# Attention over graph edges on one core: the order of TensorE's and ScalarE's work within a slot of 512 edges

## The chip, the cores and the metric

The kernel runs on one core of a Trainium2 chip. The metric is device time in microseconds (us) for one execution of the whole program, as the median over runs. Lower is better.

## What is computed

The reference is one layer of a graph model on 1250 nodes of 768 features: two rounds of graph attention (GATv2) over 41,250 edges, a linear-attention mixer and a feed-forward block. The change lies in the graph attention, of which this is the core:

```python
hs = (x @ Ws + bs).reshape(N, H, HD)
hd = (x @ Wd + bd).reshape(N, H, HD)
hs_e = hs[src]
e = jax.nn.leaky_relu(hs_e + hd[dst], SLOPE)
logits = jnp.einsum('ehd,hd->eh', e, attn)
m = jax.ops.segment_max(logits, dst, num_segments=N)
ex = jnp.exp(logits - m[dst])
s = jax.ops.segment_sum(ex, dst, num_segments=N)
alpha = ex / s[dst]
out = jax.ops.segment_sum(alpha[..., None] * hs_e, dst, num_segments=N)
```

## The kernel before, in words

The edges are sorted by destination and cut into tiles of 128. Four tiles make a macro of 512 edges, and there are 91 macros in each of the two rounds (function `attend`, called twice). Each macro passes through three steps, and the steps of three successive macros are worked on together in one slot:

- **turn** (of macro m+1): the 512 gathered source rows (`rows[b]`, 128 edges by 800 columns for each tile) are turned, so that features lie on partitions, in six chunks of 128 features. For each tile of a chunk, TensorE makes two instructions into the same 128x128 piece of a PSUM bank (`turned`): a bf16 product that places the destination's row (`dst_rows` by `place`, the "place product", L559) and a transpose of the source rows that is added to it (L561). A chunk fills a bank of 512 columns. There are four banks, so a chunk waits until ScalarE has taken the chunk four before it. ScalarE takes a chunk with a Relu into `relu[c]` (function `bend`, L502, 128x512).
- **head** (of macro m): TensorE sums the bent chunks to eight scores for each edge (`sum_heads`, L574 and L578). VectorE scans them for running maxima (`scan_left`, `scan_right`, L659 and L664) and subtracts them (`shift`, L668). TensorE turns the scores back (`turn_back`, L584), and ScalarE makes the weights of them (`weights`, L512). ScalarE also makes `rise` and `drop` (L506, L508), TensorE sums the drops (`sum_drops`, L589), and ScalarE makes the `factors` of them by which older sums shrink (L518, four instructions). VectorE spreads the weights over 1024 columns (`spread_out`, L676).
- **message** (of the macro whose head step was in the slot before): TensorE multiplies spread weights by rows (`messages`, L597), and VectorE adds the results to the sums, scaled by the factors (`add_total`, L686, eight instructions).

The order in each engine's queue is written out by hand, in a function `slot` for each engine, and it is the same in every slot. On TensorE it is: messages, chunk 0, heads, chunks 1 to 3, turn back, chunk 4, sum of drops, the linear part (L568), chunk 5. On ScalarE: bend 0, bend 1, rise and drop, weights, bends 2 to 4, factors, bend 5. On VectorE (untouched by the change): line up (L647), join (L653, two instructions), the eight adds, copy of an index, the two scans, shift, and small work, then the spreading. GpSimd gathers rows by indirect DMA (L483), and SyncE loads the places and flags.

What waits for what around the change: the adds wait for all four factors of their macro and for the earlier adds (L682 to L684); heads wait for the bends and for the joins; `turn_back` waits on TensorE's sequencer for the shift (L583); the spreading waits for the weights; the messages wait for the spreading.
Of the kernel before, what the change touches and what calls it, by code (L numbers as in the profile page):

```python
# [15 lines left out]
P = 128  # L16
# [15 lines left out]
G = 4  # L32
# [369 lines left out]
def attend(layer, ahead, sums, table, local_rows, run_flags, src_index, dst_local, first_dst, still_first, block_of, sum_of,  # L402
           iota_row, split_of, ident, head_rows, quarter_mask, dst_rows, sems, nc, **_):

    with ExitStack() as ctx:
# [32 lines left out]
        def chunk(b, c):  # L438
            return (b * KC + c) % BANKS
# [7 lines left out]
        with nc.Block() as block:  # L447
# [48 lines left out]
            @block.scalar  # L496
            def _(act):
                def bend(m, b, c, first=False):
                    if not first:
                        act.wait_ge(heads_done, m)  # L500
                    act.wait_ge(turned_done, m * KC + (c + 1))
                    act.activation(relu[c][:], turned[chunk(b, c)][:], ACT.Relu, scale=attn_size[:, c:c + 1]).then_inc(bent, 1)  # L502

                def drops(m, b):
                    act.wait_ge(scanned, m * SCANS + (SCANS + 2))
                    act.activation(rise[:], left[(b + 1) % 2][:, P - 1:P], ACT.Identity, bias=right[:, 0:1], scale=-1.0).then_inc(raised, 1)  # L506
                    act.wait_ge(raised, m + 2)
                    act.activation(drop[:], quarter_mask[:, 0], ACT.Relu, scale=rise[:]).then_inc(dropped, 1)  # L508

                def weights(m):  # L510
                    act.wait_ge(turned_back, 2 * m + 1)
                    act.activation(weight[:].rearrange("p (j h) -> p j h", j=G), back[:, 0:P].rearrange("p (j r) -> p j r", j=G)[:, :, 0:H],  # L512
                                   ACT.Exp).then_inc(weights_ready, 1)

                def factors(m, b):
                    act.wait_ge(turned_back, 2 * m + 2)
                    for j in range(G):
                        act.activation(factor[b % 2][:, j, :], back[:, P + j * HH:P + (j + 1) * HH], ACT.Exp,  # L518
                                       scale=first_dst[:, bass.ds(m * G + j, 1)]).then_inc(weights_ready, 1)

                def slot(turn, head, first=False, fresh=False):
                    if turn:
                        bend(turn[0], turn[1], 0, first)
                        bend(turn[0], turn[1], 1, first)
                    if head:
                        drops(head[0], head[1])
                        weights(head[0])
                    if turn:
                        bend(turn[0], turn[1], 2, first)
                        bend(turn[0], turn[1], 3, first)  # L530
                        bend(turn[0], turn[1], 4, first)
                    if head:
                        factors(head[0], head[1])
                    if turn:
                        bend(turn[0], turn[1], 5, first)

                act.sem_inc(bent, BANKS)  # L537
                slot(macro(0, 0), None, first=True)
                slot(macro(0, 1), macro(0, 0))
                with act.Fori(0, LOOPS) as i:  # L540
                    for b in range(UNROLL):
                        slot(macro(i, b + 2), macro(i, b + 1))
                slot(macro(LOOPS, 2), macro(LOOPS, 1))
                slot(None, macro(LOOPS, 2))
                act.wait_ge(merged, 1)
                for j in range(1, G):
                    act.activation(merge[:, j], back[:, 0:2 * G * HH].rearrange("p (s j k) -> p j s k", s=2, j=G)[:, j], ACT.Exp,
                                   scale=first_dst[:, j:j + 1]).then_inc(merge_seen, 1)

            @block.tensor  # L550
            def _(pe):
                def turn_chunk(m, b, round, at, c):
                    if c == 0:
                        pe.wait_ge(gathered[b], landed(layer, b, round + 1))
                        pe.wait_ge(place_ready, m + 1)
                    pe.wait_ge(bent, m * KC + (c + 1))
                    for j in range(G):
                        into = turned[chunk(b, c)][:, j * P:(j + 1) * P]
                        pe.matmul(into, dst_rows[0:SP_ROWS, bass.ds(at[j], 1), c * P:(c + 1) * P].rearrange("p o d -> p (o d)"),  # L559
                                  place[b][:, j * P:(j + 1) * P], start=True, stop=False)  # L560
                        last = pe.matmul(into, rows[b][:, j, c * P:(c + 1) * P], ident[:],  # L561
                                         is_transpose=True, start=False, stop=True)
                    last.then_inc(turned_done, 1)

                def turn_linear(m):
# [35 lines left out]
                def slot(turn, head, message):  # L601
                    if turn:
                        at = places_of(nc, mybir.EngineType.PE, block_of, turn[0], 1)
                    if message:
                        for pair in range(2):
                            messages(message[0], message[1], pair)
                    if turn:
                        turn_chunk(*turn, at, 0)
                    if head:
                        sum_heads(head[0], head[1])  # L610
                    if turn:
                        for c in range(1, 4):
                            turn_chunk(*turn, at, c)
                    if head:
                        turn_back(head[0])
                    if turn:
                        turn_chunk(*turn, at, 4)
                    if head:
                        sum_drops(head[0])
# [1670 lines left out]
```

## Time and profile before

| | |
|---|---|
| runs shown | 2255.08, 2255.70, 2258.92 us; median 2255.7 |
| profiled execution | span 2250.3 us from its first to its last instruction; a time of its own around that span isn't given |
| busy share | PE 96%, PEld 75%, DVE 75%, ACT 50%, POOL 40% |
| place products (L559) | 4368, two groups of 407.7 and 394.1 us busy |
| transposes (L561) | 4368, two groups of 427.9 and 413.3 us busy |
| granted TensorE clock | mean 0.986 |

PE is TensorE's array and PEld its weight loads, which overlap with it. Matmuls overlap each other, so their lengths do not add up to time: what counts is the distance from one start to the next. The letter q behind an engine's name is its sequencer, which runs ahead of the engine.

### The profile page before, as it was taken

How to read it: one execution, taken by the hardware profiler on the slowest of the kernel's cores; microseconds unless marked ns; L12 is line 12 of the kernel's file. 1: busy time of each engine (PE TensorE's matmuls, PEld its weight loads, DVE VectorE, ACT ScalarE, POOL GpSimd, SP SyncE). 2: the span in 40 equal slices, each digit the busy share in tenths (PEclk: the TensorE clock that was granted, in tenths of full speed). 3: DMA queues.
4: the chain of work that ended last, by engine and by line, in shares of the span. 5: the costliest groups of instructions: out<-in, count | busy, mean ns of one | idle time of the engine just before them, and what ended most of it. 6: DMA issues, size and time to landing. Idle time of an engine off the chain costs nothing. (4 is left out here: it accounts for less than half of the span.)

```text
span 2250.3 us, 86767 instructions
## 1 busy us (share of the span) xinstructions
PE 2154.9 (96%) x31007; PEld 1684.2 (75%) x31007; DVE 1678.2 (75%) x4435; ACT 1133.4 (50%) x2749; POOL 896.5 (40%) x849
## 2 busy tenths in 40 slices
PE   8999999998999999999997999899999999999798
PEld 4665555555888888888886655688888888888676
DVE  5546872344888888888887755588888888888884
ACT  1101200034666666666664314566666666666584
POOL 0000001022666566666652211466656656656121
PEclk9999999999999999999998999999999999999899
DMA  5002044144777777787774024587777777777421
GB/s 192 1 0 71 20 142 133 57 131 133 249 250 247 249 250 243 248 252 239 247 245 153 29 97 132 168 252 242 251 242 248 240 245 250 244 246 238 171 88 48
DMA packets 143398, 404.07 MB, mean 180 GB/s; under 512 B 21811, under 2 KB 81625, under 8 KB 143073
## 3 DMA queue, kind: packets, MB, share of 16 engines
q0 software_dynamic: 59584, 298.64, 41.0%
q1 hardware_dynamic: 79691, 93.00, 13.8%
q10 hardware_dynamic: 3828, 7.85, 1.0%
q8 instruction: 264, 4.33, 0.8%
q14 instruction: 31, 0.25, 0.0%
HBM read 370.77 MB, written 17.17 MB: 172 GB/s over the span
## 5 line engine op out<-in xcount | busy, mean ns | idle before, releaser
L502 ACT ACTIVATE at_relu<-at_turned,ah_attn_size 128x512 f32<-128x512 f32 x1092 | 716.2, 692 | 392.0 <-PE at_heads L578 363.4
L483 POOL DMA_INDIRECT at_rows<-table,ah_index x360 | 404.6, 1124 | 269.0 <-DVE ah_index L696 158.5
L483 POOL DMA_INDIRECT ah_room<-table,ah_index x352 | 399.8, 1136 | 260.8 <-DVE ah_index L696 174.3
L561 PE MATMUL at_turned<-ident,ah_room 128*128 128x128 f32 x2208 | 427.9, 280 | 2.3 <-issue 2.3
L559 PE MATMUL at_turned<-ah_place,dst_rows 96*128 96x128 bf16 x2208 | 407.7, 223 | 23.4 <-ACTq L537 19.2
L561 PE MATMUL at_turned<-ident,at_rows 128*128 128x128 f32 x2160 | 413.3, 277 | 1.7 <-issue 1.4
L559 PE MATMUL at_turned<-at_place,dst_rows 96*128 96x128 bf16 x2160 | 394.1, 222 | 2.2 <-issue 1.5
L686 DVE SCALAR_TENSOR_TENSOR sums<-sums,at_factor,at_total 128x97 f32 x1456 | 343.7, 310 | 1.4 <-DVE at_gap L751 0.7
L561 PEld LDWEIGHTS at_turned<-ident,ah_room 128*128 128x128 f32 x2208 | 318.1, 144 | 26.2 <-issue 1.7
L561 PEld LDWEIGHTS at_turned<-ident,at_rows 128*128 128x128 f32 x2160 | 307.8, 143 | 24.5 <-issue 2.2
L676 DVE TENSOR_TENSOR at_spread<-at_lined,at_weight 128x1024 f32<-128x1024 f32 x182 | 223.3, 1227 | 127.7 <-ACT at_weight L512 127.7
L559 PEld LDWEIGHTS at_turned<-ah_place,dst_rows 96*128 x2208 | 224.1, 103 | 60.6 <-issue 60.5
L653 DVE SCALAR_TENSOR_TENSOR at_relu<-at_relu,ah_pair_sign 128x512 f32<-128x512 f32 x364 | 256.3, 746 | 0.0
L559 PEld LDWEIGHTS at_turned<-at_place,dst_rows 96*128 x2160 | 217.4, 103 | 36.8 <-issue 36.6
L597 PE MATMUL at_total<-at_rows,at_spread 128*32 128x100 f32 x5760 | 144.3, 253 | 1.9 <-DVE at_spread L676 1.8
L597 PE MATMUL at_total<-ah_room,at_spread 128*32 128x100 f32 x5888 | 145.7, 251 | 0.3 <-issue 0.2
L597 PEld LDWEIGHTS at_total<-ah_room,at_spread 128*32 128x32 f32 x5888 | 125.6, 110 | 12.3 <-DVE at_spread L676 2.4
L597 PEld LDWEIGHTS at_total<-at_rows,at_spread 128*32 128x32 f32 x5760 | 124.5, 111 | 13.2 <-DVE at_spread L676 3.9
L518 ACT ACTIVATE at_factor<-at_back,first_dst 128x2 f32<-128x2 f32 x728 | 132.8, 283 | 1.1 <-PE at_back L589 1.1
L578 PE MATMUL at_heads<-at_relu,ah_sign_mask 128*8 128x128 f32 x2912 | 116.5, 273 | 1.6 <-issue 1.4
L574 PE MATMUL at_heads<-at_relu,ah_sign_mask 128*8 128x128 f32 x2912 | 114.0, 273 | 0.2 <-issue 0.2
L1748 ACT ACTIVATE pr_parts<-pr_dst_row 128x384 bf16<-128x384 f32 x60 | 31.2, 522 | 124.9 <-DVEq L1845 112.0
(317 smaller groups left out, 3179.7 us busy)
## 6 DMA issues: line engine op xcount, KB each, us to landing
at_flags<-run_flags SPq DMA_DIRECT2D x182, 64.0 KB
dst_rows<-pr_parts SPq DMA_DIRECT2D x76, 144.0 KB, 2.6
ah_place<-local_rows SPq DMA_DIRECT2D x92, 96.0 KB
at_place<-local_rows SPq DMA_DIRECT2D x90, 96.0 KB
table<-ah_room SPq DMA_DIRECT2D x20, 400.0 KB, 2.4
ah_room<-table,ah_index POOLq DMA_INDIRECT x368
at_rows<-table,ah_index POOLq DMA_INDIRECT x360
mx_w<-in_L_mix_W_qkv SPq DMA_DIRECT2D x4, 1152.0 KB, 11.8
```

The costliest lines, as they stand in the source:

```text
L483: pool.indirect_dma_start(rows[b][:, j, :], None, table, bass.IndirectOffsetOnAxis(index[b][:, j:j + 1], 0)).then_inc(gathered[b], 16)
L502: act.activation(relu[c][:], turned[chunk(b, c)][:], ACT.Relu, scale=attn_size[:, c:c + 1]).then_inc(bent, 1)
L518: act.activation(factor[b % 2][:, j, :], back[:, P + j * HH:P + (j + 1) * HH], ACT.Exp, scale=first_dst[:, bass.ds(m * G + j, 1)]).then_in ...
L559: pe.matmul(into, dst_rows[0:SP_ROWS, bass.ds(at[j], 1), c * P:(c + 1) * P].rearrange("p o d -> p (o d)"), place[b][:, j * P:(j + 1) * P], ...
L561: last = pe.matmul(into, rows[b][:, j, c * P:(c + 1) * P], ident[:], is_transpose=True, start=False, stop=True)
L574: pe.matmul(head_row(j), sign_mask[:, c, :], relu[c][:, j * P:(j + 1) * P], start=False, stop=False)
L578: last = pe.matmul(head_row(j), sign_mask[:, c, :], relu[c][:, j * P:(j + 1) * P], start=False, stop=c == JOINED[-1][1])
L597: last = pe.matmul(part(j)[h % HM * S:(h % HM + 1) * S, h // HM, :], spread[:, j, h, :], rows[b][:, j, :].rearrange("p (g h r) -> p h g r" ...
L653: dve.scalar_tensor_tensor(relu[c][:], relu[from_][:], pair_sign[:, c:c + 1], relu[c][:], ALU.mult, ALU.add).then_inc(joined, 1)
L676: dve.tensor_tensor(spread[:], lined[:].unsqueeze(2).broadcast_to([P, G, H, S]), weight[:].rearrange("p (j h) -> p j h", j=G).unsqueeze(3) ...
L686: dve.scalar_tensor_tensor(into[:, k], into[:, k], factor[b % 2][:, j, k:k + 1], part(j)[:, k, 0:HW], ALU.mult, ALU.add).then_inc(added, 1)
L1748: act.activation(heads_half(parts[t % 2][:, s, :], half), heads_half(dst_row[:], half), ACT.Copy).then_inc(split_done, 1)
```

## The change

The change does three things in `attend`. TensorE makes the four place products of a chunk in a row and then the four transposes, instead of alternating (and only the first of a bank carries the start flag). TensorE makes the heads directly behind the messages, ahead of chunk 0, and turns back behind chunk 2 instead of chunk 3. ScalarE makes bend 5 ahead of the factors instead of behind them.

```diff
@@ scalar: slot
                         bend(turn[0], turn[1], 4, first)
+                        bend(turn[0], turn[1], 5, first)
                     if head:
                         factors(head[0], head[1])
-                    if turn:
-                        bend(turn[0], turn[1], 5, first)
@@ tensor: turn_chunk
                     pe.wait_ge(bent, m * KC + (c + 1))
+                    into = [turned[chunk(b, c)][:, j * P:(j + 1) * P] for j in range(G)]
                     for j in range(G):
-                        into = turned[chunk(b, c)][:, j * P:(j + 1) * P]
-                        pe.matmul(into, dst_rows[0:SP_ROWS, bass.ds(at[j], 1), c * P:(c + 1) * P].rearrange("p o d -> p (o d)"),
-                                  place[b][:, j * P:(j + 1) * P], start=True, stop=False)
-                        last = pe.matmul(into, rows[b][:, j, c * P:(c + 1) * P], ident[:],
-                                         is_transpose=True, start=False, stop=True)
+                        pe.matmul(into[j], dst_rows[0:SP_ROWS, bass.ds(at[j], 1), c * P:(c + 1) * P].rearrange("p o d -> p (o d)"),
+                                  place[b][:, j * P:(j + 1) * P], start=j == 0, stop=False)
+                    for j in range(G):
+                        last = pe.matmul(into[j], rows[b][:, j, c * P:(c + 1) * P], ident[:],
+                                         is_transpose=True, start=False, stop=j == G - 1)
                     last.then_inc(turned_done, 1)
@@ tensor: slot
-                    if turn:
-                        turn_chunk(*turn, at, 0)
                     if head:
                         sum_heads(head[0], head[1])
                     if turn:
-                        for c in range(1, 4):
+                        for c in range(3):
                             turn_chunk(*turn, at, c)
                     if head:
                         turn_back(head[0])
                     if turn:
+                        turn_chunk(*turn, at, 3)
                         turn_chunk(*turn, at, 4)
```

On TensorE, from the messages to the heads, one slot of the kernel before reads so (ISA is the register instruction, `x16` and `x4` count equal rows):

```order
L597 MATMUL at_total1_0<-ah_room,at_spread_0 32x100 x16
L559 ISA
L559 MATMUL at_turned0_0<-at_place2_0,dst_rows 128x128
L561 MATMUL at_turned0_0<-ident,at_rows2_0 128x128
L559 ISA
L559 MATMUL at_turned0_0<-at_place2_0,dst_rows 128x128
L561 MATMUL at_turned0_0<-ident,at_rows2_0 128x128
...
L574 MATMUL at_heads_0<-at_relu4_0,ah_sign_mask 8x128 x4
L574 MATMUL at_heads_0<-at_relu5_0,ah_sign_mask 8x128 x4
```

The same place in the changed kernel (whose place products stand on line 558):

```order
L597 MATMUL at_total1_0<-ah_room,at_spread_0 32x100 x16
L574 MATMUL at_heads_0<-at_relu4_0,ah_sign_mask 8x128 x4
L574 MATMUL at_heads_0<-at_relu5_0,ah_sign_mask 8x128 x4
L578 MATMUL at_heads_0<-at_relu1_0,ah_sign_mask 8x128 x4
L578 MATMUL at_heads_0<-at_relu3_0,ah_sign_mask 8x128 x4
L558 ISA
L558 MATMUL at_turned0_0<-at_place2_0,dst_rows 128x128
...
L561 MATMUL at_turned0_0<-ident,at_rows2_0 128x128 x4
```

The heads now stand next to the messages, and each chunk has four register instructions and products ahead of four transposes. On ScalarE, from the weights to the factors in an early slot of the kernel before:

```order
L512 ACTIVATE at_weight_0<-at_back_0 128x32
L502 ACTIVATE at_relu2_0<-at_turned0_0,ah_attn_size 128x512
L502 ACTIVATE at_relu3_0<-at_turned1_0,ah_attn_size 128x512
L502 ACTIVATE at_relu4_0<-at_turned2_0,ah_attn_size 128x512
L518 ACTIVATE at_factor0_0<-at_back_0,first_dst 128x2 x4
L502 ACTIVATE at_relu5_0<-at_turned3_0,ah_attn_size 128x512
```

And in the changed kernel:

```order
L512 ACTIVATE at_weight_0<-at_back_0 128x32
L502 ACTIVATE at_relu2_0<-at_turned0_0,ah_attn_size 128x512
L502 ACTIVATE at_relu3_0<-at_turned1_0,ah_attn_size 128x512
L502 ACTIVATE at_relu4_0<-at_turned2_0,ah_attn_size 128x512
L502 ACTIVATE at_relu5_0<-at_turned3_0,ah_attn_size 128x512
L518 ACTIVATE at_factor0_0<-at_back_0,first_dst 128x2 x4
```

The four factors moved behind bend 5, which reads the last chunk that TensorE turns in the slot.

## Rows read from the trace of the kernel before

**Rows 1.** Busy time by stretch; columns: busy us of each engine, clock, DMA share, GB/s
```profile
560.00:1200.00 640.00, 635.28 (x12853) 556.78 (x12846) 560.75 (x1652) 430.15 (x1127) 392.00 (x346) 1.00 0.78 247
1440.00:2140.00 700.00, 677.01 (x13706) 592.33 (x13705) 606.87 (x1771) 461.02 (x1197) 396.24 (x354) 0.99 0.75 239
```

**Rows 2.** The same view for line 559 alone: PE and PEld busy (count)
```profile
620.00:1150.00 530.00, 315.58 (x1728) 173.95 (x1728) 1.00 0.78 247
1560.00:2050.00 490.00, 288.52 (x1581) 159.25 (x1580) 1.00 0.78 245
```

**Rows 3.** Timeline of PE over one slot: start us, length us, instruction
```profile
802.22 0.28 PE L561 MATMUL at_turned<-ident,at_rows 128*128 128x128 f32 x1
802.42 1.58 PE L597 MATMUL at_total<-at_rows,at_spread 128*32 128x100 f32 x64
803.94 0.23 PE L559 MATMUL at_turned<-ah_place,dst_rows 96*128 96x128 bf16 x1
...
804.52 0.28 PE L561 MATMUL at_turned<-ident,ah_room 128*128 128x128 f32 x1
804.73 0.62 PE L574 MATMUL at_heads<-at_relu,ah_sign_mask 128*8 128x128 f32 x16
805.17 0.62 PE L578 MATMUL at_heads<-at_relu,ah_sign_mask 128*8 128x128 f32 x16
805.73 0.23 PE L559 MATMUL at_turned<-ah_place,dst_rows 96*128 96x128 bf16 x1
...
807.65 0.22 PE L559 MATMUL at_turned<-ah_place,dst_rows 96*128 96x128 bf16 x1
807.71 0.28 PE L561 MATMUL at_turned<-ident,ah_room 128*128 128x128 f32 x1
807.82 0.27 PE L584 MATMUL at_back<-ident,at_shifted 128*128 128x128 f32 x1
807.93 0.22 PE L559 MATMUL at_turned<-ah_place,dst_rows 96*128 96x128 bf16 x1
...
808.63 0.29 PE L589 MATMUL at_back<-at_drop,head_rows 128*128 128x8 f32 x2
808.77 0.31 PE L568 MATMUL at_heads<-ident,at_linear 128*128 128x128 f32 x1
808.92 0.22 PE L559 MATMUL at_turned<-ah_place,dst_rows 96*128 96x128 bf16 x1
```

**Rows 4.** Timeline of PE near the end: six transposes of one kind in a row
```profile
2146.09 0.82 PE L2092 MATMUL fi_turned<-ident,nodes 128*128 128x128 f32 x6
```

**Rows 5.** Timeline of ACT over the slot
```profile
802.66 0.73 ACT L518 ACTIVATE at_factor<-at_back,first_dst 128x2 f32<-128x2 f32 x4
803.24 0.73 ACT L502 ACTIVATE at_relu<-at_turned,ah_attn_size 128x512 f32<-128x512 f32 x1
...
808.13 0.20 ACT L512 ACTIVATE at_weight<-at_back 128x32 f32<-128x32 f32 x1 [0.30 <-issue]
808.23 1.84 ACT L502 ACTIVATE at_relu<-at_turned,ah_attn_size 128x512 f32<-128x512 f32 x3
809.94 0.73 ACT L518 ACTIVATE at_factor<-at_back,first_dst 128x2 f32<-128x2 f32 x4
```

**Rows 6.** Timeline of DVE over the slot
```profile
802.66 1.41 DVE L653 SCALAR_TENSOR_TENSOR at_relu<-at_relu,ah_pair_sign 128x512 f32<-128x512 f32 x2
803.99 1.89 DVE L686 SCALAR_TENSOR_TENSOR sums<-sums,at_factor,at_total 128x97 f32 x8
806.84 0.29 DVE L668 TENSOR_TENSOR at_shifted<-at_heads,at_right 128x128 f32<-128x128 f32 x1
808.36 1.23 DVE L676 TENSOR_TENSOR at_spread<-at_lined,at_weight 128x1024 f32<-128x1024 f32 x1 [0.67 <-ACT at_weight L512]
```

**Rows 7.** Sequencers, by line: L683 and L686 (DVE), L583 and L559 (TensorE); last numbers: first and last start
```profile
L683 DVEq FUSED_REGOPS  x1: 46/46/46, 803.5 to 803.5; - x1
L686 DVEq FUSED_REGOPS  x4: 57/60/64, 803.6 to 804.1; - x4
L583 PEldq EVENT_SEMAPHORE  x1: 51/51/51, 807.2 to 807.2; - x1
L559 PEldq FUSED_REGOPS  x4: 46/46/46, 807.3 to 807.8; - x4
L559 PEldq FUSED_REGOPS  x12: 46/46/46, 805.0 to 806.4; - x12
```

## The prediction

> **What bounds the kernel now.** First the stretches: in the two attention rounds (about 1340 of 2250 us) PE is busy 635 of 640 and 677 of 700 us, DVE 88%, ACT 67%, and DMA 78%, at full clock [rows 1]. So TensorE's order decides there. Then the length of a slot. A slot has 24 place products, so the counts of line 559 give 72 slots in 530 us and 65.9 in 490 us, or 7.36 and 7.44 us each [rows 2]. The timeline of an undisturbed slot has 7.28 us: it starts with the messages at 802.42 and its last chunk, as long as the others, ends 0.78 us behind 808.92, at 809.70 [rows 3]. The difference, some 0.12 us a slot or 22 us over 182 slots, is scattered pauses that the change doesn't touch.
>
> I write times within the slot from its messages (0.00). TensorE [rows 3]: messages 0.00, chunk 0 at 1.52, heads 2.31, chunk 1 at 3.31, turn back 5.40, chunk 4 at 5.51, drops 6.21, linear 6.35, chunk 5 at 6.50, next slot 7.28. DVE [rows 6]: joins 0.24 to 1.65, eight adds 1.57 to 3.46, shift done 4.71, then 0.67 us idle until the spreading at 5.94 (done 7.17, just ahead of the next messages). ACT [rows 5]: weights at 5.71, bends 2 to 4 end 7.65, factors 7.52 to 8.25, that is 0.24 to 0.97 of the next slot, where the adds use them at 1.57.
>
> **Heads behind the messages: a gain on PE.** A start-to-start distance of 0.21 us stands between the last transpose and the heads (804.52 to 804.73), and as much between transpose and messages, where a transpose is otherwise followed after 0.11 (807.71 to 807.82) [rows 3]. The change of shape thus costs about 0.1 us, and there are four in a slot. Heads next to messages leave two. I take 0.1 off at the first (heads at 1.42) and 0.1 for the chunk that no longer ends in a change: 0.2 us a slot. Bounds: 0.1, if going from 32 columns to 8 costs as much as the others, and 0.2.
>
> **Place products in a row: a small gain.** A pair takes 0.174 us (0.06 from place product to transpose, 0.114 from there to the next) and a chunk 0.695 [rows 3]. Six like transposes in a row start (0.82-0.27)/5 = 0.11 us apart [rows 4]. Nothing shows a place product behind another; it can hardly take longer than the 0.06 to a transpose whose weights are larger. With 0.056 to 0.06, a chunk takes 0.67 to 0.695 us. I take 0.675. [...]
>
> If PE were all that counts, the slot would be 7.28 - 0.2 - 6x0.02 = 6.96 us.
>
> **Bend 5 ahead of the factors: a new loop.** Bend 5 reads chunk 5, the last of TensorE's slot. Its last transpose starts 0.20 ahead of the next messages and lasts 0.28 (802.22) [rows 3], so it is done at 0.08 of the next slot. Bend 5 starts at about 0.11 and takes 0.69 (it was one of three in 1.84, which overlap a little [rows 5]): it ends at 0.80. The four factors start 0.12 ahead of that, as they do behind bend 4 (808.23+1.84 against 809.94), and take 0.73: done at **1.41**, not 0.97. In exchange nothing is won: the heads read bend 5 at 1.42 at the earliest and had it at 1.55 when they stood at 2.31 [rows 3, 5].
>
> The adds wait for all four factors, and this wait stands in DVE's sequencer (L683), which passed it at 803.5, with the first register instruction of the adds 0.1 later and another 0.1 until an add can start [rows 7]. So the first add starts at 1.41+0.03+0.2 = **1.64**, where it was 1.57. It can't be earlier however early the joins end. Behind it nothing changes on DVE: from the first add to the end of the shift are 807.13-803.99 = 3.14 us [rows 6]. The shift is done at 4.78, and what is queued behind the adds (index copy, scans) is as late.
>
> **Turn back behind chunk 2: a new wait.** TensorE arrives there at 2.42 (heads 1.42, as long as before 1.00) + 3x0.675 = 4.45, against 5.40 before. The wait for the shift stands in TensorE's sequencer (L583), which passed it at 807.2, less than 0.1 behind the end of the shift at 807.13 [rows 6, 7]. With 0.04 it is released at 4.82. Before, there were 0.66 us from this release to the turn back at 807.82, in which the sequencer made the next register instructions. Now there is nothing between. These come 0.125 us apart (eleven distances in 1.4 us [rows 7]), more slowly than place products run (0.06), and in a row none is hidden behind a transpose. The four of chunk 3 come 0.125 to 0.50 behind the release, and the fourth product can't start before its register instruction has run (0.046 us, and as much again for the way to the engine, my estimate): 4.82+0.59 = 5.41. The engine alone would have been there at 4.45+0.11+0.17 = 4.73. So PE stands still for about 0.68 us a slot in two pieces, before the turn back and in the place products of chunk 3. In other chunks the sequencer is ahead: it has the heads' 1.00 us to prepare chunk 0.
>
> Sum: fourth product 5.41, rest of chunk 3 0.06+3x0.11+0.114 = 0.50, chunk 4 0.675, drops and linear 0.29, chunk 5 0.675, change of shape 0.09: the next slot starts at **7.64**. The other loop (turn back 4.93, weights by 5.5, spreading done 6.75) isn't late. Each slot hands the same times to the next, so this holds throughout: +0.36 us a slot.
>
> About 178 slots have all three steps: +64 us. Part of the 22 us of pauses falls before the turn back, where PE now waits anyway (4.45 of 7.28 of the slot); about 10 us of them are swallowed. Net +54 us, on a span of 2250.3. The median of the runs is 5.4 above this span, and I keep that: 2255.7+54 = **2310 us**. Work outside the rounds isn't touched. The gathers are triggered by the index copy, 0.07 later in a longer slot, and get more time, so DMA costs nothing; it is at 78% and falls.
>
> **The rivals.**
> - *The sequencer's pitch does not show.* Register instructions without transposes between them may go through faster than 0.125 us. Then only the wait for the shift is left: turn back at 4.93, and 0.11+3x0.675+0.29+0.09 behind it gives 7.45. +0.17x178 = 30, less 10: about 2276. For it: nothing shows four register instructions with a single product between them. Against: they kept 0.125 whatever lay between.
> - *PE stays the bound* (the other side): the slot is then 6.96 to 7.1 and the kernel 32 to 57 us faster, 2199 to 2224. Place and price: this decides at the first add. If it started 0.6 us earlier than I have it, at about 1.0, the release would come at 4.2 and TensorE would find its instructions ready. For it: DVE has 0.67 us of idle time per slot, which an earlier turn back turns into earlier joins. Against: the joins don't decide; the factors do, and they can't be done before 1.41 as they stand behind a bend that stands behind chunk 5.
> - *The halves cancel*: a slot of 7.2 to 7.3, if the factors come sooner than I count and the pitch shows only partly. Within 0.2% of before, about what a measurement of this kernel can tell from no change.
> - *Place products in a row are slow.* By the worst bound that a row gives (0.11 us each, as a transpose), chunks 4 and 5 grow by 3x0.055 each: 7.97 a slot, some 2369. Nothing in the rows supports it, as a product after a product loads less. [...]
>
> **How the numbers follow.** The forecast as worked out has 0.52 (2295 to 2325, with add, release and chunk each off by a few hundredths), the unseen pitch 0.22, slow place products 0.06: slower 0.80. PE as the bound 0.14, cancelling 0.06. The range leaves out the faster cases and the slowest: 2266 to 2327.
>
> **What would show it.** Right: slots of about 7.6 us; in ACT's timeline the factors directly behind bend 5 and done 1.4 behind the messages; the first add 1.6 behind them, with DVE idle before it and released by ACT's factors; idle PE before the turn back and in chunk 3, released by DVE's shift or "issue"; the spreading no longer just ahead of the messages; PE's share below 93% in the rounds. Wrong: adds at 1.3 or earlier, PE without idle time before the turn back, or slots under 7.28. Apart from the sum, heads 1.42 behind the messages and chunks of 0.675 would confirm the two small gains.

## The result, and the profile after

The changed kernel takes 2312.85 us (median of 4 runs, 2311.01 to 2314.47) against 2256.64 us before in the same comparison: a ratio of 1.0248 (95% interval 1.0232 to 1.0264). It is slower by 56 us; the forecast was 2310 us. The profiled execution has a span of 2312.5 us.

The busy time by stretch, with the columns of [rows 1]; the second line starts later, as the whole second round does:

```profile
560.00:1200.00 640.00, 605.78 (x12259) 540.82 (x12257) 536.46 (x1568) 429.83 (x1073) 419.76 (x331) 1.00 0.79 235
1480.00:2180.00 700.00, 657.23 (x13239) 585.89 (x13241) 586.43 (x1723) 466.69 (x1166) 438.45 (x349) 1.00 0.76 226
```

PE was busy 635 of the first 640 us [rows 1] and is now busy 606, or 95%. It has gained idle time, at an unchanged granted clock of 1.00. The same view for the line of the place products, as in [rows 2]:

```profile
620.00:1150.00 530.00, 175.92 (x1648) 129.59 (x1648) 1.00 0.79 235
1560.00:2050.00 490.00, 162.38 (x1516) 119.44 (x1516) 1.00 0.79 236
```

24 products make a slot, so 68.7 and 63.2 slots: 7.72 and 7.76 us each, where it was 7.36 and 7.44. Over 182 slots these are 62 us, as much as the spans of the two profiled executions differ (2312.5 against 2250.3): the whole loss lies in the slots of the two rounds.

PE's timeline over one undisturbed slot, to be laid beside [rows 3] (undisturbed means without a scattered pause; `...` stands for rows left out):

```profile
1064.42 0.61 PE L561 MATMUL at_turned<-ident,at_rows 128*128 128x128 f32 x4
1064.95 1.58 PE L597 MATMUL at_total<-at_rows,at_spread 128*32 128x100 f32 x64
1066.35 0.62 PE L574 MATMUL at_heads<-at_relu,ah_sign_mask 128*8 128x128 f32 x16
...
1067.34 0.40 PE L558 MATMUL at_turned<-ah_place,dst_rows 96*128 96x128 bf16 x4
1067.57 0.60 PE L561 MATMUL at_turned<-ident,ah_room 128*128 128x128 f32 x4
1068.02 0.39 PE L558 MATMUL at_turned<-ah_place,dst_rows 96*128 96x128 bf16 x4
...
1069.89 0.30 PE L584 MATMUL at_back<-ident,at_shifted 128*128 128x128 f32 x1 [0.37 <-DVE at_first_max L670]
1070.03 0.58 PE L558 MATMUL at_turned<-ah_place,dst_rows 96*128 96x128 bf16 x4
1070.44 0.61 PE L561 MATMUL at_turned<-ident,ah_room 128*128 128x128 f32 x4
1070.89 0.39 PE L558 MATMUL at_turned<-ah_place,dst_rows 96*128 96x128 bf16 x4
...
1072.60 0.29 PE L597 MATMUL at_total<-at_rows,at_spread 128*32 128x100 f32 x4
```

Both small gains are there: the heads start 1.40 behind the messages, and a chunk takes 0.67 to 0.68 (1067.34 to 1068.02), later 0.66. Then the turn back comes at 4.94, with idle PE before it. The row of four place products behind it takes 0.58 us instead of 0.39: this is the second piece of standstill. No idle column shows it, since each product lasts 0.22 us and the next starts 0.12 us behind it. The slot is 1072.60 - 1064.95 = 7.65 us. It is one of the shorter ones: of the 67 whole slots between 620 and 1150 us the median is 7.71, and the longer ones differ mostly in that same row, which takes up to 0.1 more.

The profile names `at_first_max` as what the turn back waited for. That is the instruction behind the shift on DVE; the shift itself ended at 1069.74 (below), and the wait was passed at 1069.8. Over the window of 620 to 1150 us the waits view has this row, and the kernel before has none such:

```profile
PE at_back L584 <- DVE at_first_max L670: 19.9, 54, 0.4
```

ACT's and DVE's timelines of that slot:

```profile
1065.06 0.69 ACT L502 ACTIVATE at_relu<-at_turned,ah_attn_size 128x512 f32<-128x512 f32 x1 [0.27 <-PE at_turned L561]
1065.65 0.71 ACT L518 ACTIVATE at_factor<-at_back,first_dst 128x2 f32<-128x2 f32 x4
```

```profile
1064.33 1.41 DVE L652 SCALAR_TENSOR_TENSOR at_relu<-at_relu,ah_pair_sign 128x512 f32<-128x512 f32 x2
1066.60 1.90 DVE L685 SCALAR_TENSOR_TENSOR sums<-sums,at_factor,at_total 128x97 f32 x8 [0.86 <-PE at_total L597]
1069.45 0.29 DVE L667 TENSOR_TENSOR at_shifted<-at_heads,at_right 128x128 f32<-128x128 f32 x1
1070.45 1.22 DVE L675 TENSOR_TENSOR at_spread<-at_lined,at_weight 128x1024 f32<-128x1024 f32 x1
```

Bend 5 waits for PE's last transpose (0.11 behind the messages), and the factors are done at 1.41. DVE has finished its joins at 0.8 and sits idle for 0.86 us. Its adds start at 1.65 and the shift ends at 4.79. The profile puts that idle time down to PE's messages (at_total). The sequencers' rows say otherwise:

```profile
L681 DVEq ALU_OP  x1: 40/40/40, 1065.9 to 1065.9; - x1
L682 DVEq FUSED_REGOPS  x1: 46/46/46, 1066.4 to 1066.4; - x1
L583 PEldq EVENT_SEMAPHORE  x1: 51/51/51, 1069.8 to 1069.8; - x1
L558 PEldq FUSED_REGOPS  x4: 46/46/46, 1069.9 to 1070.3; - x4
```

None of DVE's rows is a wait itself, so when a wait was passed is read from the first row behind it. Behind the wait for the messages' first half (line 679) that is L681. It starts at 0.97, 0.07 us behind the end of the last message of that half, in all 67 whole slots between 620 and 1150 us. Behind the wait for the factors (line 681) it is L682. It starts at 1.44 or 1.45, 0.04 us behind the end of the last factor (1066.36 in this slot), in all 67, and the first add follows 0.21 us later. So the factors came last. On TensorE the wait for the shift has a row of its own, L583, which starts 0.04 us behind the end of the shift in 66 of the 67 slots, here at 1069.8. The four register instructions of chunk 3 come only behind it, the first 0.13 us later. In the same window no two register instructions of L558 start less than 0.12 us apart, and no place product starts less than 0.10 us behind its own. The fourth product of chunk 3 stands at this limit, 0.10 us behind its register instruction in the median slot.

### The profile page after: what moved, and what is told of

It reads as the page before. It is cut to its first block and busy times, and to the rows that moved or that the text cites. A ratio compares the mean times of both kernels' runs of the same rounds, so it can differ in the third digit from the quotient of the medians.

```text
span 2312.5 us, 86767 instructions
## 1 busy us (share of the span) xinstructions
PE 2157.4 (93%) x31007; PEld 1708.0 (74%) x31007; DVE 1683.8 (73%) x4435; ACT 1178.4 (51%) x2749; POOL 991.2 (43%) x849
## 5 line engine op out<-in xcount | busy, mean ns | idle before, releaser
L483 POOL DMA_INDIRECT ah_room<-table,ah_index x352 | 449.0, 1275 | 247.3 <-DVE ah_index L695 163.1
L561 PE MATMUL at_turned<-ident,ah_room 128*128 128x128 f32 x2208 | 338.1, 276 | 0.8 <-issue 0.8
L561 PE MATMUL at_turned<-ident,at_rows 128*128 128x128 f32 x2160 | 327.6, 274 | 0.0
L558 PE MATMUL at_turned<-ah_place,dst_rows 96*128 96x128 bf16 x2208 | 237.7, 221 | 20.1 <-ACTq L536 19.3
L561 PEld LDWEIGHTS at_turned<-ident,ah_room 128*128 128x128 f32 x2208 | 235.1, 142 | 1.0 <-issue 0.9
L558 PE MATMUL at_turned<-at_place,dst_rows 96*128 96x128 bf16 x2160 | 231.3, 220 | 1.8 <-issue 1.2
L561 PEld LDWEIGHTS at_turned<-ident,at_rows 128*128 128x128 f32 x2160 | 227.7, 141 | 0.0
L558 PEld LDWEIGHTS at_turned<-ah_place,dst_rows 96*128 x2208 | 175.1, 99 | 58.1 <-issue 42.7
L558 PEld LDWEIGHTS at_turned<-at_place,dst_rows 96*128 x2160 | 170.0, 98 | 38.7 <-issue 23.7
L584 PE MATMUL at_back<-ident,at_shifted 128*128 128x128 f32 x182 | 53.9, 296 | 58.9 <-DVE at_first_max L670 58.4
```

The source lines that it names most:

```text
L483: pool.indirect_dma_start(rows[b][:, j, :], None, table, bass.IndirectOffsetOnAxis(index[b][:, j:j + 1], 0)).then_inc(gathered[b], 16)
L558: pe.matmul(into[j], dst_rows[0:SP_ROWS, bass.ds(at[j], 1), c * P:(c + 1) * P].rearrange("p o d -> p (o d)"), place[b][:, j * P:(j + 1) * ...
L561: last = pe.matmul(into[j], rows[b][:, j, c * P:(c + 1) * P], ident[:], is_transpose=True, start=False, stop=j == G - 1)
L584: pe.transpose(back[:, 0:P], shifted[:], ident[:]).then_inc(turned_back, 1)
```

## The experiments

State of the theory before them. **A**: the slot is set by a loop: last chunk, bend 5, factors, adds, scans, release of the turn back, then the sequencer's pitch, then the rest of the chunks. **B**: turning back behind chunk 2 is too early for VectorE, whatever ScalarE does. **S**: the register instructions don't matter, only the wait.

### 1. Bend 5 behind the factors again (in the changed kernel)

```diff
-                        bend(turn[0], turn[1], 5, first)
                     if head:
                         factors(head[0], head[1])
+                    if turn:
+                        bend(turn[0], turn[1], 5, first)
```

> The changed kernel with bend 5 behind the factors again, all else as changed. Theory A (the loop chunk 5, bend 5, factors, adds, scans, turn back decides): the factors are done about 0.5 us behind the messages, the adds start as soon as the joins are done, the release of the turn back moves from 4.8 to about 4.4 and the slot falls from 7.64 to about 7.1 us: 2216 to 2235 us. Rival B (turning back behind chunk 2 is too early for VectorE whatever ScalarE does, the bend's place is without effect): the first add stays near 1.6, slots of 7.5 us or more, 2285 us or more.

Measured: 2263.38 us, ratio to before 1.0027 (1.0016 to 1.0037), in neither of the expected ranges. The place of one activation is worth 49 us of the 56. B alone is refuted. But the gain that A promised beyond that did not come. The slot from 959.36 to 966.61 has 7.25 us and not 7.1. The rows of PE, DVE and DVE's sequencer there:

```profile
959.36 1.58 PE L598 MATMUL at_total<-at_rows,at_spread 128*32 128x100 f32 x64
963.98 0.27 PE L585 MATMUL at_back<-ident,at_shifted 128*128 128x128 f32 x1
966.61 0.29 PE L598 MATMUL at_total<-at_rows,at_spread 128*32 128x100 f32 x4
```

```profile
960.62 1.89 DVE L686 SCALAR_TENSOR_TENSOR sums<-sums,at_factor,at_total 128x97 f32 x8 [0.31 <-PE at_total L598]
...
963.46 0.29 DVE L668 TENSOR_TENSOR at_shifted<-at_heads,at_right 128x128 f32<-128x128 f32 x1
```

```profile
L682 DVEq ALU_OP  x1: 40/40/40, 960.3 to 960.3; - x1
```

The joins end at 0.94 and the factors earlier, yet the adds start at 1.26. Now it is the wait for the messages' first half that comes last: the first row behind it (L682 in this kernel) starts at 0.965 in all 70 whole slots of the window, 0.07 us behind the end of that half, while the factors are done at 0.45 in the median. I had left it out: the adds have a floor at 1.26, so the release has one at 4.44, and 2.8 us behind it make 7.25. The loop is still there, with the messages as its first member in place of bend 5 and the factors. In this slot TensorE itself came late (turn back at 4.62 with no wait, behind a row of place products in chunk 0 that took 0.62 us). In 52 of the 70 whole slots of the window the turn back stands at 4.54 to 4.56, just behind the release. The first add stands at 1.26 or 1.27 in all of them, and no slot is shorter than 7.25.

### 2. Turn back behind chunk 3 (in the changed kernel)

```diff
-                        for c in range(3):
+                        for c in range(4):
                             turn_chunk(*turn, at, c)
                     if head:
                         turn_back(head[0])
                     if turn:
-                        turn_chunk(*turn, at, 3)
                         turn_chunk(*turn, at, 4)
```

> The changed kernel with the turn back behind chunk 3 instead of chunk 2; bend 5 stays ahead of the factors. Both theories have TensorE arrive at about 5.05, behind the release at 4.8. Theory A with the sequencer's pitch: adds still at 1.62 and the shift still at 4.79, but they are covered now. Bound by turn back to messages over weights and spreading (1.88 us): slots of 6.94 us, 2190 to 2205 us, some 110 us faster than the changed kernel and some 55 faster than the kernel before. If bend 5 costs by itself, without a wait at the turn back, the slot stays above 7.2: 2245 us or more.

Measured: 2238.18 us, ratio 0.9908 (0.9892 to 0.9925), 75 us faster than the changed kernel and 33 us above the expected range. The late factors, which are still there, don't hold the kernel up any more; they cost together with a turn back that comes before the release. The best slots are near the expected 6.94 (messages at 919.31 and 926.31, 7.00 us), but the mean is 530/(1740/24) = 7.31 us. The missing 40 us are in the difference between the two, and it has two parts. One is scattered pauses, which experiments 5 to 11 take up. The other is the sequencer's pitch again. The turn back stands at 5.07, at most 0.24 behind the release (4.83), so the register instructions of the row behind it aren't all ready: the fourth starts 0.27 us behind the turn back in the median slot, where the first product starts 0.11 us behind it. In 51 of the 71 whole slots of the window the fourth place product of that row starts 0.21 us or more behind the first, where 0.17 is normal, and the median slot has 7.14 us.

### 3. Place products and transposes in alternation again (in the changed kernel)

The diff is abbreviated; `[...]` stands for addresses that stay as they are.

```diff
                     for j in range(G):
-                        pe.matmul(into[j], dst_rows[...], place[b][...], start=j == 0, stop=False)
-                    for j in range(G):
-                        last = pe.matmul(into[j], rows[b][...], ident[:], is_transpose=True, start=False, stop=j == G - 1)
+                        pe.matmul(into, dst_rows[...], place[b][...], start=True, stop=False)
+                        last = pe.matmul(into, rows[b][...], ident[:], is_transpose=True, start=False, stop=True)
```

> The changed kernel with place product and transpose in alternation again, order of chunks, heads, turn back and bends as changed. With the sequencer's pitch of 0.125 us: the row of place products of chunk 3 no longer stands still, which gives back more than the rows had won: turn back at 4.93, then 2.58 us: slots of 7.52 us, about 2291 us, faster than the changed kernel by about 20. Without such a pitch the rows were a plain gain and taking them back makes slots of 7.70 to 7.78: 2325 to 2340 us.

Measured: 2292.21 us, ratio 1.015 (1.0133 to 1.0167): 20 us faster than the changed kernel, as the pitch demands. PE behind the turn back:

```profile
710.40 0.30 PE L583 MATMUL at_back<-ident,at_shifted 128*128 128x128 f32 x1 [0.30 <-DVE at_first_max L669]
710.53 0.22 PE L558 MATMUL at_turned<-at_place,dst_rows 96*128 96x128 bf16 x1
...
711.06 0.22 PE L558 MATMUL at_turned<-at_place,dst_rows 96*128 96x128 bf16 x1
711.12 0.28 PE L560 MATMUL at_turned<-ident,at_rows 128*128 128x128 f32 x1
711.23 0.22 PE L558 MATMUL at_turned<-at_place,dst_rows 96*128 96x128 bf16 x1
```

A pair takes 0.175, more than the pitch of 0.125 (in none of the fourteen traces do two register instructions of the place products start less than 0.12 us apart between 620 and 1150 us), so chunk 3 runs through in 0.70 us (710.53 to 711.23), where the row version took 0.86 (1070.03 to 1070.89). Rows are a gain of 0.02 to 0.035 a chunk where the sequencer is ahead, and a loss of 0.16 right behind a release. S is refuted: the wait is the same, and only the register instructions have come to stand between transposes.

### 4. The wait for the shift on the weight load

```diff
-                    pe.wait_ge(weights_ready, m * EXPS + EXPS)
                     pe.wait_ge(scanned, m * SCANS + (SCANS + 3))
+                    pe.wait_ge(weights_ready, m * EXPS + EXPS)
```

> The changed kernel with the two waits of the turn back written in the other order, so that the wait for the shift lies on the weight load in the engine's queue, and the sequencer can run ahead of it with its register instructions. If the sequencer's standstill costs the second piece: turn back still at about 4.9, but chunk 3 runs at 0.66 us behind it and the slot falls from 7.64 to about 7.43: 2272 to 2282 us. If the register instructions are not what the place products of chunk 3 wait for: no change, 2308 to 2316 us.

Measured: 2295.39 us, ratio 1.0156 (1.0139 to 1.0173). It gives 17 us instead of the expected 31 to 41. The sequencer's rows and the turn back itself:

```profile
L583 PEldq EVENT_SEMAPHORE  x1: 51/51/51, 633.6 to 633.6; - x1
L558 PEldq FUSED_REGOPS  x5: 46/46/46, 634.8 to 635.3; - x5
```

```profile
634.84 0.33 PE L584 MATMUL at_back<-ident,at_shifted 128*128 128x128 f32 x1 [0.28 <-DVE at_shifted L667]
```

The other wait, written last now, has the row L583. It was passed early, at 633.6. The wait for the shift has no row: its release shows only in the weight load and the transpose of the turn back, which both start at 634.84, 0.06 us behind the end of the shift (0.15 us in the changed kernel). The register instructions still begin only with the turn back, at 634.8, and in 59 of the 69 whole slots of the window the first of them starts 0.01 us ahead of it. That first one has a wait of its own, for a bend, but that bend was done some 4 us before. So in this place too the wait for the shift held the sequencer; my premise that it could run ahead was wrong. What is saved is the semaphore instruction (51 ns) between the release and the turn back, which stands at 4.85 instead of 4.94, and little of the row's standstill (0.53 us, where it was 0.58).

### 5 to 8. Each part alone, and a version built from them

The three parts were put into the kernel before, one at a time. Bend 5 ahead of the factors, alone (the first piece of the diff of the change):

> The kernel before with bend 5 ahead of the factors and nothing else. By the theory so far the first add moves from 1.57 to 1.62 and the shift from 4.71 to 4.79, but the turn back stands at 5.40 there, so both are covered: slots of 7.28 us, 2252 to 2262 us, no change. If the late factors cost by themselves: slots longer by 0.05 or more, 2266 us or more.

Measured: 2261.04 us, ratio 1.0015 (1.0005 to 1.0026): 3 us, hardly clear of noise. The delay is covered, as expected, though it is larger than I had it: over the window the median first add stands at 1.80, not 1.62, since bend 5 there has to wait for bend 4 and ends at 0.94, not at 0.80, and the factors are done at 1.55, not at 1.41. The shift ends at 4.94, still ahead of the turn back at 5.40.

Place products in rows, alone (the second piece):

> The kernel before with the place products of a chunk in a row and nothing else. A chunk takes 0.66 instead of 0.695 (0.055 from place product to place product). The turn back then stands at 5.26, and the spreading, 1.88 from turn back to messages, becomes the last: slots of 7.14 us. That is 25 us less; pauses of the sequencer may give 5 to 10 of them back: 2234 to 2248 us. If rows were bad for the sequencer everywhere, not only behind a late release: 2256 us or more.

Measured: 2252.19 us, ratio 0.9976 (0.9963 to 0.9989). The shortest slots are as expected (7.15 us), the time is 4 us above the range.

Heads behind the messages, chunks 0 to 3 behind them, alone:

> The kernel before with the heads directly behind the messages, chunks 0 to 3 and the turn back behind them, and nothing else (pairs, factors ahead of bend 5). Two changes of shape less are 0.2 us: turn back at 5.20, slots of 7.08 us; 36 us less, of which longer pauses take 5 to 10: 2224 to 2238 us. If going from the messages' shape to the heads' costs as much as the others, 0.1 us: slots of 7.18, 2240 to 2248 us.

Measured: 2251.17 us, ratio 0.9965 (0.9951 to 0.9978), outside both expected ranges. Both are gains, but only a fifth to a quarter of what undisturbed slots promise. These are as short as expected (7.06 us for the heads, in PE's timeline from 715.57 to 722.63). Changing from the messages' shape to the heads' costs nothing: the first head starts 0.066 us behind the last message, as a group of four messages does behind the group before it (0.066 in the median), where the first message starts 0.207 behind the transpose ahead of it. The mean slot is 530/(1708/24) = 7.45 us. PE's waits in the window of 620 to 1150 us name most of the difference of some 28 us:

```profile
PE at_turned L559 <- issue: 7.2, 11, 1.2
PE at_turned L561 <- issue: 6.0, 9, 1.2
PE at_heads L578 <- issue: 2.5, 5, 1.0
PE at_heads L574 <- issue: 1.8, 5, 0.6
```

That is 17.5 us of pauses in which PE waited for nothing that the profile shows; the kernel before had 3.1 in the same window (1.9, 0.8, 0.2 and 0.2).

**Turn back within chunk 3.** With heads first, rows, and the factors ahead of bend 5, turning back can be placed between the release (about 4.6) and the point from which weights and spreading would be last (4.99, my estimate: a slot of 6.87 for PE alone, less the 1.88 from turn back to messages):

```diff
@@ turn_chunk
                     for j in range(G):
+                        if j == 2 and between is not None:
+                            turn_back(between)
                         last = pe.matmul(into[j], rows[b]...
@@ slot
                         for c in range(3):
                             turn_chunk(*turn, at, c)
+                        turn_chunk(*turn, at, 3, head[0] if head else None)
-                    if head:
+                    elif head:
                         turn_back(head[0])
                     if turn:
-                        turn_chunk(*turn, at, 3)
                         turn_chunk(*turn, at, 4)
```

It has the bend order of experiment 1 and the order of waits of experiment 4 as well, so its gain isn't that of the new place alone. (The diff is against the changed kernel and abbreviated.)

> A version meant to be better than both: heads behind the messages, place products in rows, factors ahead of bend 5, and the turn back between the second and third transpose of chunk 3, with its wait for the shift written first. Turn back at 4.85, adds from 1.4, release at 4.6, so the rows of chunk 4 are prepared; turn back to messages 1.88 is 6.73, PE alone 6.87: undisturbed slots of 6.9 us. With the pauses that the run with the turn back behind chunk 3 had: 2210 to 2228 us. If TensorE arrives too early there as well, undisturbed slots stay at 7.1 and more, 2245 us or more.

Measured: **2210.62 us, ratio 0.9804 (0.9777 to 0.9832)**: between 1.7 and 2.2% faster than before and 102 us faster than the changed kernel, at the lower end of the expected range. PE's timeline:

```profile
708.42 1.58 PE L600 MATMUL at_total<-at_rows,at_spread 128*32 128x100 f32 x64
...
713.05 0.39 PE L564 MATMUL at_turned<-ident,ah_room 128*128 128x128 f32 x2
713.27 0.27 PE L587 MATMUL at_back<-ident,at_shifted 128*128 128x128 f32 x1
713.38 0.38 PE L564 MATMUL at_turned<-ident,ah_room 128*128 128x128 f32 x2
713.60 0.39 PE L559 MATMUL at_turned<-ah_place,dst_rows 96*128 96x128 bf16 x4
...
715.32 0.38 PE L600 MATMUL at_total<-at_rows,at_spread 128*32 128x100 f32 x8
```

The turn back stands at 4.85 with no idle time before it, and the row behind it takes 0.39 us. The slot is 6.90. In 72 of the 73 whole slots of the window that row is unhindered, against 20 of 71 in experiment 2: the shift ends at 4.54, 0.64 ahead of the row, where it ended 0.33 ahead of it there (4.85 and 5.18), and the sequencer has the time that it lacked: the fourth register instruction starts 0.21 us ahead of the row here, and 0.16 us behind its first product there.

### 9 to 11. Are the pauses waits for fetched instructions behind the gathers?

Two theories: **F**, the pauses are waits for instructions that DMA fetches, and the gathers' traffic makes them; **S** (not the S of experiments 1 to 4), they come from the sequencer's own work and don't depend on DMA. In three kernels, two of the four gathers of a macro move 64 columns instead of 800, so that the sums are formed from incomplete rows (the part in angle brackets is abbreviated):

```diff
+                        if paced and j > 1:
+                            pool.indirect_dma_start(rows[b][:, j, 0:64], None, <the table as rows of 64>, <the same index>)
```

> The kernel before, but two of the four gathers of a macro move 64 columns instead of 800 (from other rows of the table, so the outputs are not the reference's). TensorE's, ScalarE's and VectorE's instructions are the same; the gathers move little more than half. Theory F: the scattered pauses of TensorE are waits for its instructions, which are fetched by the same DMA engines as the gathers, and are seen where they are longer than the lead of the sequencer. Then they nearly vanish: slots of 7.28 us on average instead of 7.38 to 7.44, 2238 to 2250 us. Rival S: the pauses come from the sequencer's own work and don't depend on DMA: 2253 to 2262 us.

> The kernel with the heads alone moved (the run of 2251 us, undisturbed slots of 7.05 but 22 us of pauses in a window of 530 us), with the same light gathers. Theory F: the pauses fall below 5 us in the window, mean slot 7.1, 2205 to 2222 us. Rival S: pauses stay, 2240 us or more.

> The kernel with the turn back within chunk 3 (2210.6 us), with the same light gathers. Theory F: undisturbed slots of 6.89 us stay, pauses fall from 15 to below 5 us in the window: 2170 to 2188 us. Rival S: 2203 us or more.

| kernel | time with full gathers, us | with light gathers, us | DMA share, full and light | PE waits for issue in 530 us, full and light |
|---|---|---|---|---|
| before | 2258.96 | 2253.68 | 0.78, 0.51 | 3.1, 3.7 |
| heads alone | 2251.17 | 2239.23 | 0.79, 0.51 | 17.5, 13.8 |
| turn back within chunk 3 | 2210.62 | 2195.50 | 0.83, 0.56 | 12.4, 8.5 |

With light gathers the three ratios to before are 0.9987 (0.9973 to 1.0002), 0.9914 (0.9883 to 0.9946) and 0.9719 (0.9686 to 0.9751). The kernel before lies in the range of S; the two others lie between the ranges. (Their expectations put the pauses at 22 and 15 us, which was the mean slot less the undisturbed one over the window.) Taking away a third of the DMA load removes a fifth to a third of the pauses in the two faster orders and none in the kernel before. So the load of the gathers has a share at most.

F's other half, the fetching, can be looked for in the traces themselves, since the profile has a DMA queue that it calls instruction. The profile of the heads alone:

```profile
q8 instruction: 265, 4.34, 0.8%
```

These are 265 packets of 16 KB each, one in about 6 us during the rounds (92 in 530 us of the kernel before). All fourteen traces together have 343 of PE's waits for issue (those above 0.15 us) in the windows of 620 to 1150 and 1560 to 2050 us. In 340 of them PE goes on 1.2 to 1.7 us behind the landing of such a packet, although by chance it could be anything up to 6 us; the waits for the shift in the changed kernel end anywhere from 0.0 to 6.7 us behind one. That fits waits for fetched instructions and doesn't fit S, though no experiment here changed the fetching itself. A packet takes about as long with light gathers as with full ones (1.01 us against 1.04 in the heads alone, 1.09 against 1.07 in the best version, in the first window), which fits that the lighter load helped little.

The pauses grow when the messages and the heads stand together (17.5 us) and when rows take the place of pairs (8.7 us with rows alone, against 3.1). Why the same instructions in another order wait for their packets more often stays open.

### 12. Turn back behind chunk 2, alone (in the kernel before)

```diff
-                        for c in range(1, 4):
+                        for c in range(1, 3):
                             turn_chunk(*turn, at, c)
                     if head:
                         turn_back(head[0])
                     if turn:
+                        turn_chunk(*turn, at, 3)
                         turn_chunk(*turn, at, 4)
```

> The kernel before with the turn back behind chunk 2 instead of chunk 3 and nothing else (pairs, chunk 0 ahead of the heads, factors ahead of bend 5). TensorE arrives at 4.71. VectorE's adds can start at 1.25, when the first half of the messages is through, so the release can move to 4.45 to 4.6; a pair runs no faster than the sequencer, so nothing stands still behind it: undisturbed slots of 7.28, 2252 to 2264 us, no change. If turning back that early costs by itself, slots of 7.4 and more, 2275 us or more.

Measured: 2283.66 us, ratio 1.0114 (1.008 to 1.0148). I expected no change; the time lies in the other range, that of an early turn back that costs by itself. PE, then DVE, in a slot of 7.45 us (689.81 to 697.26):

```profile
692.56 0.62 PE L578 MATMUL at_heads<-at_relu,ah_sign_mask 128*8 128x128 f32 x16
694.66 0.30 PE L584 MATMUL at_back<-ident,at_shifted 128*128 128x128 f32 x1
```

```profile
691.07 1.90 DVE L687 SCALAR_TENSOR_TENSOR sums<-sums,at_factor,at_total 128x97 f32 x8
693.25 0.48 DVE L660 TENSOR_TENSOR_SCAN at_left<-at_flags,at_left,at_heads 128x128 f32<-128x128 bf16 x1 [0.20 <-PE at_heads L578]
```

The adds did start early, at 1.26, and end at 3.16. But the scan reads the heads, and these end at 692.56+0.62 = 693.18, 3.37 in the slot. The scan can't start before 3.44, which is when it started in the kernel before. So without moving the heads, an early turn back waits for them: TensorE would be there at 4.71 and turns back at 4.85. These 0.14 us, and 0.03 more from the turn back to the next place product, make the slot of 7.45 out of 7.28.

## Why the prediction was right

It was right in its mechanism, and in size closer than its terms deserve. By its own steps:

- **Heads behind the messages**: said 1.42, measured 1.40. The lower bound of 0.1 us didn't come into play.
- **Rows**: said 0.675 a chunk, measured 0.66 to 0.68. A product follows a product after 0.055 to 0.06 us (three distances of a row of 0.39 whose last product lasts 0.22). So the case of slow place products, 0.11 us apart (0.06), is refuted.
- **Bend 5**: start 0.11, factors done 1.41, both as said. Experiment 1 shows that this step carries 49 of the 56 us.
- **First add**: said 1.64, measured 1.65; **shift** 4.78 against 4.79; **turn back** 4.93 against 4.94.
- **Standstill in chunk 3**: fourth product said at 5.41, so the transposes at 5.47; the transposes start at 5.49. Experiment 3 shows the cause, and the case without the pitch (2276 us, 0.22) is refuted.
- **Slot**: 7.64 against 7.65 in an undisturbed slot, but 7.71 in the median, since the row behind the turn back is often slower than counted. Times 178, less 10 us that the pauses were to give back: 54 us said, 56 measured. That the sum is right to 2 us is partly luck: it had neither the longer rows nor the growth of the pauses.
- **PE stays the bound** (0.14): it was refused because the adds could not start at 1.0. The refusal holds, but for a reason I did not have complete. Experiment 1 took the factors away and the adds stopped at 1.26 on the messages' first half; experiment 12 shows a third guard, the heads, for the scan. I had looked only at the guard that was last in my own sum.
- **Pauses**: 22 us over the rounds, "which the change doesn't touch", of which 10 would be swallowed. The changed kernel's time came out near enough, but its waits for issue rose from 3.1 to 7.0 us in the window. As a general premise it is wrong: in the faster orders they grow to several times that.
- **Signs**: three of those named did not come. PE's share was to fall below 93% and is 95 and 94% in the two stretches, and no idle time shows in chunk 3, because part of the standstill lies under the lengths of products and transposes and counts as busy. And DVE's idle time was to be released by ACT's factors, but the profile names PE's messages; only the sequencer's rows show the factors. The others came, the spreading among them: it ends at 1071.67, 0.93 ahead of the next messages.

So the loss came from a combination. Bend 5 alone costs 3 us. Turning back earlier with heads moved, rows, and factors in their old place costs next to nothing (1.0027). Together they cost 56, and 20 of these are the rows, a gain elsewhere.

## What to carry to other kernels

Moving a consumer earlier on the bound engine gains only as far as its producer's chain is early too: list every wait on that chain (here the factors at 1.41, the messages' first half with adds at 1.26, the heads with a scan at 3.44), since taking away the last only uncovers the next. On a queue written in order, an operation put behind a wait inherits it: the factors behind bend 5, which waits for TensorE's last chunk, were done at 1.41 instead of 0.97. And the instructions with run-time addresses needed the sequencer to be ahead here: a row of four took 0.58 us right behind the late wait and 0.39 elsewhere. Right behind such a wait, put work that needs few of them, or the wait in the middle of a run of transposes as in experiment 8, where the row took 0.39.

## What the hardware showed that I had not expected

- In experiment 4 the wait for the shift, which has no row of its own there, held TensorE's sequencer as well: register instructions behind it began at 634.8, with the turn back. Elsewhere they run ahead of the engine, by 0.7 us for chunk 1 in [rows 7] (805.0 against 805.73).
- Pauses of PE "by issue" depend on the order of the same instructions: 3.1, 7.0, 12.4 and 17.5 us in 530 us for the kernel before, the changed one, the best and the heads alone. They took up to four fifths of a computed gain (36 us computed for the heads alone, 7 measured), and nearly every one (340 of 343) ends 1.2 to 1.7 us behind the landing of a packet of the queue called instruction.
- The waits view named the messages for 53.6 us of DVE's idle time that the sequencer's rows put down to the factors.
